# Diffusion stage: end rows copied from the sums' buffers, the boundary sum two places earlier, first gathers of a step spread

## What is computed

```
x = layernorm(x + gat(gat(x)))            # two attention convolutions
x = layernorm(x + attention over edges(x))
x = layernorm(x + gated edge MLP(x))
h = silu(x @ W_in.T + b_in)
out = term = h
for i in 1..6:
    term = segment_sum(term[src], dst) / max(deg, 1) / i
    out = out + term
x = layernorm(x + out @ W_out.T + b_out)
```

## Time and profile before

| | |
|---|---|
| median of the runs | 3865.31 us |
| the profiled execution | 3845.83 us |
| its span | 3844.1 us |
| PE, PEld, DVE, ACT, POOL busy | 85%, 68%, 73%, 49%, 54% |
| TensorE tile sums (L2812) | 360.0 us busy, x1200 |
| gathers of messages (L621) | 306.5 and 308.0 us busy, x300 each |

### The profile page before, as it was taken

The page is one execution under the profiler, slowest core; times in us unless marked ns, Lnnn a source line. Parts: engine busy times, 40 slices in busy tenths (PEclk is TensorE's granted clock), DMA queues, the critical chain, the costliest instruction groups (busy, mean ns, idle before and its releaser), DMA issues. The chain is left out here.

```text
span 3844.1 us, 56581 instructions
## 1 busy us (share of the span) xinstructions
PE 3249.5 (85%) x14868; PEld 2617.9 (68%) x14868; DVE 2816.0 (73%) x7894; ACT 1883.4 (49%) x5403; POOL 2085.0 (54%) x2118
## 2 busy tenths in 40 slices
PE   5999925588577799666999997999999999999875
PEld 4888824477465466333777775888878787878664
DVE  5666758699588466695666665898989898989742
ACT  3777715466333111132333332566666666666555
POOL 3667600376277566233333332767767676767567
PEclk8999969899799899755999998999999999999998
DMA  4788739644277222175333333887868686868665
GB/s 139 242 247 248 237 108 321 194 131 129 68 219 208 87 88 87 30 219 157 101 115 108 118 107 98 239 236 212 251 201 251 198 250 203 252 200 248 198 215 167
DMA packets 677311, 684.76 MB, mean 178 GB/s; under 512 B 73152, under 2 KB 631284, under 8 KB 676896
## 3 DMA queue, kind: packets, MB, share of 16 engines
q1 hardware_dynamic: 592456, 484.44, 40.4%
q0 software_dynamic: 68160, 181.21, 17.4%
q10 hardware_dynamic: 16380, 15.49, 1.2%
HBM read 401.66 MB, written 283.11 MB: 178 GB/s over the span
## 5 line engine op out<-in xcount | busy, mean ns | idle before, releaser
L2812 PE MATMUL s_i_bank<-s_i_messages,s_i_equal 128*128 128x256 f32 x1200 | 360.0, 383 | 5.6 <-DMA s_i_messages<-h,table_row 5.4
L621 POOL DMA_INDIRECT s_i_messages<-h,table_row x300 | 306.5, 1022 | 98.5 <-issue 78.7
L621 POOL DMA_INDIRECT s_i_messages<-h,table_row_b x300 | 308.0, 1027 | 90.1 <-issue 79.7
L931 POOL TENSOR_TENSOR n_powers<-n_powers,neg_half 128x8 f32<-128x8 f32 (+3 forms) x164 | 268.4, 1637 | 160.2 <-DVE n_powers L896 116.1
L856 ACT ACTIVATE n_z<-gamma_bc,n_powers 128x256 f32<-128x256 f32 x320 | 175.0, 594 | 362.0 <-POOL n_powers L931 362.0
L815 PE MATMUL s_n_bank<-w,n_xt 128*128 128x256 f32 x1280 | 305.7, 382 | 16.7 <-DMA n_xt<-in_x_t 16.7
L833 PE MATMUL s_n_bank<-w_out,n_ht 128*128 128x256 f32 x1280 | 313.9, 390 | 4.7 <-ACT n_ht L843 4.4
L824 PE MATMUL s_n_bank<-n_x3t,w_in 128*128 128x256 f32 x1280 | 302.5, 379 | 0.0
L2841 DVE SCALAR_TENSOR_TENSOR s_i_y<-s_i_bank,s_i_scale,acc 128x256 f32<-128x256 f32 x600 | 285.1, 476 | 0.3 <-PE s_i_bank L2812 0.2
L833 PEld LDWEIGHTS s_n_bank<-w_out,n_ht 128*128 128x128 f32 x1280 | 249.0, 196 | 46.2 <-ACT n_ht L843 11.1
L815 PEld LDWEIGHTS s_n_bank<-w,n_xt 128*128 128x128 f32 x1280 | 245.2, 192 | 51.3 <-DMA n_xt<-in_x_t 17.1
(11 more groups left out here) (448 smaller groups left out, 9244.8 us busy)
## 6 DMA issues: line engine op xcount, KB each, us to landing
h<-s_i_y SPq DMA_DIRECT2D x600, 128.0 KB, 3.9
n_xt<-in_x_t SPq DMA_DIRECT2D x160, 256.0 KB
out<-n_w SPq DMA_DIRECT2D x160, 256.0 KB
s_i_equal<-eq_tab SPq DMA_DIRECT2D x600, 64.0 KB, 3.9
x<-s_x_rows SPq DMA_DIRECT2D x100, 256.0 KB
out<-s_a_hs SPq DMA_DIRECT2D x100, 128.0 KB, 3.0
proj_dst<-s_a_hd SPq DMA_DIRECT2D x100, 128.0 KB
h<-s_h_rows SPq DMA_DIRECT2D x50, 256.0 KB, 3.7
```

The costliest lines, as they stand in the source:

```text
L621: return net.nc.gpsimd.indirect_dma_start(out, None, table, bass.IndirectOffsetOnAxis(index, 0))
L931: self.nc.gpsimd.tensor_tensor(v[:, 8 + b0:8 + b1], v[:, b0:b1], self.net.neg_half[:, 0:b1 - b0], ALU.pow).then_inc(self.powered, 1)
L2812: nc.tensor.matmul(banks[r % 4][:, 0:D], EQ[q % NM][:], M[q % NM][:], start=True, stop=True).then_inc(summed, 1)
```

## The change

`places` puts the boundary of a step seven places from its end instead of five. SyncE stores a tile one place behind its sum instead of two, and with each store it sends rows 0 and 1 of the buffer `Y` straight to the tile's row of `EF`; both transfers raise the same semaphore, so that each use of a buffer counts 32. The reload from `h` goes, with its semaphore. TensorE waits, ahead of the boundary product, for all ten store semaphores. GpSimd scatters the boundary one place behind it as before, but the gathers of the next step are allowed only two places later and up to eight tiles; it issues one in a place and two in the third place of each turn, so five a turn (in the first eight places of the stage still two).

```diff
--- before.py
+++ after.py
@@ -2689,7 +2689,7 @@
         g0, g1 = gaps * s // STEPS, gaps * (s + 1) // STEPS
         for t in range(T):
             at[g0 + t * (g1 - g0 - 9) // T] = (s, t)
-        at[g1 - 5] = (s, T)
+        at[g1 - 7] = (s, T)
     assert len(at) == STEPS * (T + 1)
     return at
 
@@ -2716,8 +2716,8 @@
         B = st.sb("i_bound", [T, D])
         scale = st.sb("i_scale", [P, STEPS, T])
         got, eq_in, stored = st.sem("i_gathered", NM), st.sem("i_eq_loaded", NM), st.sem("i_stored", NY)
-        scale_ready, summed, added, ends_in, scattered = (
-            st.sem(f"i_{n}") for n in ("scale_ready", "summed", "added", "ends_loaded", "scattered"))
+        scale_ready, summed, added, scattered = (
+            st.sem(f"i_{n}") for n in ("scale_ready", "summed", "added", "scattered"))
         assert T % NM == 0 and T % NY == 0
         TURNS = dn.units + 5
         GAPS = TURNS * dn.PIECES
@@ -2741,20 +2741,15 @@
                 sp.wait_ge(added, nth(s, t))
                 row = base[(s + 1) % 2] + t * P
                 sp.dma_start(net.h[row:row + P, :], Y[q % NY][:]).then_inc(stored[q % NY], 16)
-
-            def load_ends(s):
-                for b in range(NY):
-                    sp.wait_ge(stored[b], 16 * (T // NY) * (s + 1))
-                row = base[(s + 1) % 2]
-                sp.dma_start(EF[:], net.h[row:row + R, :].rearrange("(t p) d -> t p d", p=P)[:, 0:2, :]).then_inc(ends_in, 16)
+                sp.dma_start(EF[t:t + 1, :, :], Y[q % NY][0:2, :]).then_inc(stored[q % NY], 16)
+
+
             n = itertools.count()
 
             def gap():
                 i = next(n)
-                if i - 2 in at and at[i - 2][1] < T:
-                    store(*at[i - 2])
-                    if at[i - 2][1] == T - 1:
-                        load_ends(at[i - 2][0])
+                if i - 1 in at and at[i - 1][1] < T:
+                    store(*at[i - 1])
                 if i in at and at[i][1] < T:
                     load_eq(at[i][0] * T + at[i][1] + AHEAD)
             for u in range(2):
@@ -2788,8 +2783,11 @@
                     s, t = at[i - 1]
                     if t == T:
                         put_bound(s)
-                    upto_q = min((s + 1) * T if t < T else STEPS * T, s * T + t + AHEAD + 1)
-                for k in range(2):
+                    else:
+                        upto_q = min((s + 1) * T, s * T + t + AHEAD + 1)
+                if i - 3 in at and at[i - 3][1] == T and at[i - 3][0] + 1 < STEPS:
+                    upto_q = (at[i - 3][0] + 1) * T + AHEAD
+                for k in range(2 if i < AHEAD or i % dn.PIECES == 2 else 1):
                     if fetched < upto_q:
                         get(fetched)
                         fetched += 1
@@ -2804,7 +2802,8 @@
                 if r >= 4:
                     pe.wait_ge(added, r - 3)
                 if t == T:
-                    pe.wait_ge(ends_in, 16 * (s + 1))
+                    for b in range(NY):
+                        pe.wait_ge(stored[b], 32 * (T // NY) * (s + 1))
                     nc.tensor.matmul(banks[r % 4][0:T, 0:D], net.upper[:], EF[:, 0, :], start=True, stop=True).then_inc(summed, 1)
                 else:
                     pe.wait_ge(eq_in[q % NM], 16 * (q // NM + 1))
@@ -2837,7 +2836,7 @@
                     V.tensor_tensor(B[:], banks[r % 4][0:T, 0:D], EF[:, 1, :], ALU.add).then_inc(added, 1)
                 else:
                     if q >= NY:
-                        dve.wait_ge(stored[q % NY], 16 * (q // NY))
+                        dve.wait_ge(stored[q % NY], 32 * (q // NY))
                     V.scalar_tensor_tensor(Y[q % NY][:], banks[r % 4][:, 0:D], scale[:, s, t:t + 1], acc[:, t, :], ALU.mult, ALU.add).then_inc(added, 1)
             n = itertools.count()
```

## The result

The changed kernel is slower, by half a per cent. The forecast was 3847.3 us; the rival "SyncE becomes the bound" (3895, chance 0.11) is the one that happened.

A forecast was written before the change was run, and what follows sets the result against it. Between boundaries TensorE was taken to set the pace, 7.34 us a turn, so only the step boundaries could be won: 3 x 3.8 + 2 x 3.3 = 18.0 us off the 3865.31 median gives 3847.3, range 3831 to 3861.

The forecast's parts named there:

- SyncE becomes the bound: Rival: 14 issues a turn don't fit into SyncE's 7.34 us; at 0.7 a copy +30 us, 3895; chance 0.11.
- The copies: On SyncE, four more issues a turn at 0.47 us, 1.88 in all, fit into 2.47 us idle; booked at 0.
- Stores one place earlier: On SyncE, longer waits of stores for VectorE's sums come out of its idle time; booked at 0.
- The reload goes, the wait goes to TensorE: At the boundary TensorE waits for last store and copy; its ten waits lie inside the stall: 0.
- Even boundaries: After steps 0, 2, 4: wait of 3.1 us stays, five gathers between powers instead of eight; gain 3.8 us each.
- Odd boundaries: After steps 1 and 3: TensorE idle 3.5 us, low clock, yet powers come earlier; gain 3.3 us each.
- Three turns of 8.1: Behind each boundary, POOL's five gathers plus powers take 8.1 us for three turns, against TensorE's 7.34.
- Sum: Whole kernel: three even boundaries at 3.8 and two odd at 3.3 us, a gain of 18.0 us.
- Drain: End of step 5: last powers freed from the scatter, last O at low clock; 0, between -1.2 and +1.2 us.
- Longer wait: Rival: at five boundaries last store and copy land later, 12 to 18 us lost; 3862, no change; chance 0.10.
- Refill costs nothing: Rival: the whole second stall behind each boundary and its low clock go, gain 33 us; 3832; chance 0.06.
- Burst not cured: Rival: first gather still waits for the scatter, powers as late as before; 3868, no change; chance 0.03.

The follow-up runs named there:

- after_reload: The changed kernel without the copies, the ends reloaded from memory behind the last store; ratio 1.0001 to the kernel before the change.
- after_pairs: The changed kernel with one equality load for two tiles, 12 SyncE issues a turn instead of 14; 3847.16 against 3863.80 us before the change, ratio 0.9956.

## Why the prediction was wrong, point by point

**The copies, booked at 0 (wrong, the step that failed).** "Nearest row: the same kind of small copy in the MLP stage, 0.42 us and 0.47 to the next start." It was not the same kind: it goes to memory. The change's copy takes 0.565 us, 0.61 to the next start, and four take 2.44 of SyncE's 2.47 idle instead of 1.88. The neighbours didn't help enough: the equality load fell from 0.447 to 0.396. The prediction named 0.62 as the point from which SyncE decides, and that was too high as well. Its 2.47 is the idle time of one turn, and its mean of 2.66 counts the waits at the boundaries too (the longest is 12.2 us). The mean in the middles is 2.21. With 0.2 us a turn won at the loads, that puts the point at about 0.59 (an estimate, (2.21 - 0.04 + 0.2)/4), under the measured 0.61. So SyncE's turn is longer than 7.34 in the mean, which TensorE, full at 7.34, never makes up. The rival's price of 48 us in the middle, less 18, was +30; measured are +25.6 in the middle, +12.6 at the ends, and less 18.5 in the refill. It missed that the ends suffer too. The rows of before had two warnings, a row that was not of the same kind and a margin of 0.6 in 7.34. The rival had the margin; it deserved more than 0.11. Its reason, issues of over 1 us, is the smaller part: 12 turns of 102 hold one.

**Stores one place earlier, 0 (right).** In after_reload and after_pairs, which keep it, middle turns are 7.346 in the median and the middles as before.

**The reload goes, the wait goes to TensorE (right).** L2807 waits for the last copy; no further wait shows.

**Even boundaries (3.8 each, measured more).** In after_pairs end and refill together are 6.1, 5.8 and 5.3 us shorter than in the first profile of before, 4.2, 4.4 and 4.8 shorter than in the second. Right: no gather waits for the scatter, 8.1 us from powers to powers, L679's wait down to 5.3 us in the changed kernel. Off: TensorE waits 2.15, 2.22 and 3.01 us at L2807, not 3.1, since the last copy at 2608.70 has landed 2.5 us later, and at all three the clock stays up (L2807 0.65). In the changed kernel, with SyncE late, the wait was 3.36 and the P behind it fell to the low clock (2.86), as forecast.

**Odd boundaries (3.3 each, measured 0.2 to 2.0).** Here the step was too hopeful. The wait of 3.5 came out as 2.98 and 2.89 in after_pairs (4.42 and 3.54 in the changed kernel), and the low clock is there:

```profile
2821.52 1.14 PE L2807 MATMUL s_i_bank<-s_i_ends,upper 100*100 100x256 f32 x2 [4.42 <-DMA s_i_ends<-s_i_y]
...
2822.03 3.32 PEld L833 LDWEIGHTS s_n_bank<-w_out,n_ht 128*128 128x128 f32 x8
```

What was off is the number of slow turns. "Three turns of 8.1" holds behind even boundaries: tile to tile 8.15, 8.17, 8.15. Behind odd ones there are four: 7.82, 8.43, 8.15 and 8.89, 3.9 us over the pace where the even ones lose 2.4. The prediction carried the even case over to them. It also priced the low clock for one group, and in after_pairs it lasts for two, O and H:

```profile
2816.18 3.32 PEld L833 LDWEIGHTS s_n_bank<-w_out,n_ht 128*128 128x128 f32 x8
2819.59 2.80 PEld L824 LDWEIGHTS s_n_bank<-n_x3t,w_in 128*128 128x128 f32 x8
```

That is 6.1 us for 2.9 + 1.7, so 1.5 more, and the next powers come as much later: 11.6 us behind the start of L2807 instead of 10.2. One sign of being right fails here: the first gather does wait for the scatter, 2.07 us. It costs nothing by itself, since POOL is idle again for 3.44 us ahead of those powers.

**Sum (18.0; near for the boundaries).** Over five boundaries after_pairs is 18.9 us shorter than the first profile of before and 15.6 than the second; the medians say 16.6. The forecast was too low at the even boundaries and too high at the odd ones, and the two cancel: that the sum fits is luck in part. **Drain, 0:** the last middle is 131.3 us in both.

**The other rivals.** Longer wait (3862): its effect is there in the changed kernel, +12.6 at the ends, but from a late queue: with two issues a turn fewer it goes. Refill costs nothing (3832): not so with eight tiles of lead; with six ahead only part of it remains and the kernel comes to 3830. Burst not cured: refuted.

## What to carry to other kernels

Price an added DMA issue by a row of the same form: where both of its ends lie mattered more here than its size. Then add up the whole turn of the queue, by means and not by medians, against the turn of the engine that sets the pace. Check a count of waits against the idle time in the timeline before you divide by it. Something paid at each of 600 tiles outweighs what is won at five boundaries, so make room in the queue first (two equality tiles in one load did) and then add. When a change has three parts, one of them may be most of the gain: here it was one line about the gathers, 0.9964 by itself, against 0.9956 for all three parts with room in the queue. The intervals of the two overlap; the stages differ by 4.8 us.

## What the runs showed of the hardware

- An issue on SyncE costs more for a copy from chip to chip than for one from chip to memory: 0.565 against 0.311 us for the same two rows. Half the bytes took 0.503. A load from memory to chip took 0.30 (200 KB) to 0.447 (64 KB), so it isn't the on-chip target alone.
- The profile shows SyncE's own waits in part: 157 and 36 of one kind in two profiles of the same kernel with the same idle times.
- The price of an issue depends on its neighbour: the equality load, 0.447 us before, takes 0.320 behind a copy to memory, 0.396 behind a two-row copy on chip and 0.579 behind a one-row copy. Why is open; nothing here looks inside an issue. The Trainium skill, "DMA: Bandwidth & Descriptors", Why a DMA increments its semaphore by 16 and not by 1, says that a transfer on fewer than 16 engines has the remaining increments written by the issuing sequencer, and that the number of engines comes from the slowest dimensions of both sides. By that rule the two-row copies to memory and on chip are alike, two engines each; the measured 0.311 and 0.565 are not, so it isn't what makes the difference.
- The same page, Issuing engines are not separate DMA queues, calls the time that a sequencer takes to start a DMA "usually small relative to the DMA itself". For the single store this trace agrees: 0.466 us of issue against 3.9 to landing. But the issues of one queue add up: fourteen of them filled a turn of 7.6 us, while the DMA share was 0.83, where before it was 0.83 to 0.85.
- L2807 ran at 1.15 us after 2.98 us of idle time and at 0.65 after 3.36: idle time alone did not tell the clock of the next products in these rows.
- Open is also what moves the stage's start between 2403 and 2424 us in code that no kernel here changes.
